# Mask products over 64 contraction rows, the base product split at column 256, lora's first product ahead of the attention values, mixing bias loaded group by group

## What is computed

```python
x = x + attn(cond(x, cond_128))          # per-sequence 32x32 mixing of tokens, then attention
x = x + ffn(conv(x, cond_128, fside))    # grouped conv of 9 taps, then a dense layer with lora experts

# cond: softmax of a small network of cond_128 weighs 8 matrices: out = agg_w @ x + agg_b
# attn: q, k, v = x @ Wq, x @ Wk, x @ Wv; rope on q and k; 32 query heads, 8 key heads of 16;
scores = jnp.einsum('bkgqd,bkmd->bkgqm', qg, k) / np.sqrt(HEAD_DIM)
scores = jnp.where(causal, scores, -jnp.inf)
out = jnp.einsum('bkgqm,bkmd->bkgqd', softmax(scores), v);  out @ Wo
# ffn:
base_out = jnp.einsum('btd,od->bto', x, base_W) + base_b
w = weights of the 8 best of 15 router classes, mapped to 8 experts
h = jnp.einsum('btd,erd->bter', x, A)
lora = jnp.einsum('bter,eor->bto', h * w[..., None], B) * 2
```

## Time and profile before

| | us |
|---|---|
| median of 3 runs | 644.11 |
| lowest, highest | 641.46, 644.9 |
| profiled execution, its own time | 646.57 |
| its span in the trace | 644.6 |

### The profile page before, as it was taken

How to read it: one execution, slowest core, us unless ns; L and a number is a source line. 1 busy time by engine, 2 the same in 40 slices (tenths; PEclk the granted TensorE clock), 3 DMA queues, 4 the chain that set the end, 5 groups by cost and what they waited for, 6 DMA issues and landing times.

```text
span 644.6 us, 14143 instructions
## 1 busy us (share of the span) xinstructions
PE 608.1 (94%) x4928; PEld 504.9 (78%) x4928; DVE 477.1 (74%) x1201; ACT 227.1 (35%) x635; POOL 223.8 (35%) x181
## 2 busy tenths in 40 slices
PE   4977996999999999999999999999999999999885
PEld 3665775888888888888888888888888888888664
DVE  3556565788778787878877878787887787878743
ACT  4342332333333343334333334333433333433310
POOL 6253131443333333344333333334433333333310
PEclk9979797999999999999999999999999999999989
DMA  7746346444344455444344445544533344444430
GB/s 172 123 133 135 88 105 152 124 116 108 88 95 104 102 122 122 122 122 122 97 99 92 100 102 122 122 122 122 122 96 99 90 102 103 122 122 106 107 82 34
DMA packets 121446, 71.23 MB, mean 110 GB/s; under 512 B 48357, under 2 KB 103301, under 8 KB 121176
## 3 DMA queue, kind: packets, MB, share of 16 engines
q1 hardware_dynamic: 119952, 70.53, 44.9%
q10 hardware_dynamic: 1336, 0.24, 0.2%
q0 software_dynamic: 144, 0.28, 0.2%
HBM read 51.49 MB, written 19.53 MB: 110 GB/s over the span
## 4 chain that ended last, share of the span: by engine, by line
PE 86%; DMA 5%; DVE 5%; issue 2%; SPq 1%; ACT 1%; POOL 0%; ACTq 0%; DVEq 0%
PE ps L415 20%; PE ps L566 15%; PE ps L593 9%; PE ps L587 8%; PE ps L613 5%; PE ps L605 5%; PE ps L515 4%; PE ps L632 4%; PE ps L552 4%; PE ps L654 3%; PE ps L621 2%; PE ps L577 2%; DMA scratch<-x_dram 2%; PE ps L555 1%; PE ps L601 1%
## 5 line engine op out<-in xcount | busy, mean ns | idle before, releaser
L941 POOL TENSOR_TENSOR qk<-network,t 128x640 f32<-128x640 f32 x31 | 48.3, 1558 | 161.7 <-DVE t L1118 161.7
L415 PE MATMUL ps<-wqkv_hi,y_hi 128*128 128x512 f32 (+1 forms) x256 | 89.4, 349 | 8.5 <-POOL y_lo L933 7.0
L415 PE MATMUL ps<-wqkv_hi,y_lo 128*128 128x512 f32 (+1 forms) x256 | 88.7, 346 | 0.0
L415 PE MATMUL ps<-wqkv_lo,y_hi 128*128 128x512 f32 (+1 forms) x256 | 88.5, 346 | 0.0
L953 POOL TENSOR_TENSOR raw<-x1p,basebB 128x512 f32<-128x512 f32 x32 | 49.3, 1541 | 64.9 <-DVE x1p L1193 64.9
L745 ACT ACTIVATE raw<-ps 128x512 f32<-128x512 f32 x64 | 37.8, 595 | 76.0 <-PE ps L632 75.9
L415 PEld LDWEIGHTS ps<-wqkv_hi,y_hi 128*128 128x128 f32 x256 | 49.7, 194 | 17.1 <-DVE raw L1137 9.2
L964 DVE TENSOR_TENSOR oT_lo<-ps,oT_hi 128x256 fp32r<-128x256 f32 x64 | 24.2, 419 | 50.4 <-ACT oT_hi L745 50.4
L948 POOL TENSOR_TENSOR raw<-raw,zero 128x512 f32<-128x512 f32 x32 | 33.2, 1039 | 79.6 <-DVE raw L1182 79.6
L807 ACT ACTIVATE raw<-raw 128x512 f32<-128x512 f32 x64 | 40.4, 632 | 54.9 <-DVE raw L1137 54.9
L925 POOL TENSOR_TENSOR raw<-raw,rz 128x512 f32<-128x512 f32 x32 | 33.6, 1049 | 65.6 <-DVE rz L1147 65.6
(11 more groups left out here) (182 smaller groups left out, 1485.4 us busy)
## 6 DMA issues: line engine op xcount, KB each, us to landing
scratch<-x_dram SPq DMA_DIRECT2D x96, 256.0 KB, 4.8
x_dram<-x1p SPq DMA_DIRECT2D x32, 260.0 KB, 2.1
xm<-x SPq DMA_DIRECT2D x32, 256.0 KB, 3.8
xr<-x SPq DMA_DIRECT2D x32, 256.0 KB, 2.7
out<-raw SPq DMA_DIRECT2D x32, 256.0 KB, 2.1
v_dram<-vS SPq DMA_DIRECT2D x32, 64.0 KB
vB<-v_dram SPq DMA_DIRECT2D x128, 16.0 KB, 4.2
mixb<-mixb_dram SPq DMA_DIRECT2D x1, 1280.0 KB, 7.7
```

The costliest lines, as they stand in the source:

```text
L415: last = mm(dst, a, b, start=(n == 0), stop=(n == 3 * len(left) - 1))
L941: nc.gpsimd.tensor_tensor(qk[:, :], t1, t2[:, :], ALU.add).then_inc(qk_sb, 1)
```

## The change

- The mask products use 64 contraction rows; DVE fills the 32 added rows of `query16` with zeros at the start.
- `BASE6` is 256: 12 products of 400 columns come first, then 12 of 256. DVE's adds follow these widths: `route2` adds 256 columns, `output` 256 and 256.
- `lora`'s first product (256 columns) becomes `lora_first`, between `conv` and `values`; the waits of `values` stand ahead of it. The product of 2 columns is gone. The other five stay after `values`.
- DVE copies the second half of `oT_hi`, ACT the first.
- `rawbase` is loaded ahead of the values of step 0; `prepare_base` (0, 1) moves to step 0 and (2, 3) to the place after `scores` in step 1.
- ACT and DVE split the router and A weights (`prepare_ar`) at the head of step 0; ACT copies the values there too, and starts Wo's split after `y_hi`, not ahead of the queries.
- `load_mixw(4, G)` moves from the end of step 0 to the end of step 1. `late_bias` is replaced by a load of 128 values per group, two steps ahead of its use, with a wait for the count in `next_y`.

The core of the diff:

```diff
-BASE6 = 3 * P
+BASE6 = 2 * P
...
             sp.dma_start(mixb[:, P:4 * P], mixb_row[P:4 * P].partition_broadcast(P)).then_inc(mixb_in, 16)
+            sp.dma_start(rawbase, baseW.rearrange("(p j) l -> p j l", j=PH)).then_inc(ld["base"], 16)
...
-            def late_bias(lo, hi):
+            def load_bias(u):
...
-                if peeled(t, 0):
+                if peeled(t, 1):
                     sp.wait_ge(mixw_out, 16)
                     load_mixw(sp, 4, G, mixw_in)
-                if peeled(t, 1):
-                    late_bias(4, 12)
-                if peeled(t, 2):
-                    late_bias(12, G)
+                if live(t + 3) and (not isinstance(t, int) or t > 0):
+                    load_bias(t + 3)
...
+            def lora_first(u):
                 pe.wait_ge(hwT_hi_sb, u + 1)
                 pe.wait_ge(hwT_lo_sb, u + 1)
+                if live(u + 2):
+                    values_ready(u + 2)
+                mm(ps[:, 6, 0:BASE6], hwT_hi[:, :], lora_hi[:, 0:BASE6], start=False, stop=False)
...
-                    rows = slice(h * P // 2, h * P // 2 + S)
+                    rows = slice(h * P // 2, (h + 1) * P // 2)
                     mm(ps[:, h, :], query16[rows, :], causal16[rows, :], start=True, stop=False)
...
-                if not isinstance(t, int):
-                    mm(ps[0:S, 4, 0:2], convW[:, 0, :, :].rearrange("p j o -> p (j o)"), xc[:, 0, 0:2], start=True, stop=True)
...
-                if peeled(t, 1):
+                if peeled(t, 0):
                     pe.wait_ge(prep_sb, 1)
                     prepare_base((0, 1))
+                if peeled(t, 1):
+                    prepare_base((2, 3))
...
-                if peeled(t, 1):
-                    pe.wait_ge(oT_lo_sb, 2)
-                    prepare_base((2, 3))
...
-                    for a in range(2):
-                        last = copy(heads(oT_hi, a), heads_ps(a))
-                    last.then_inc(oT_hi_sb, 1)
+                    copy(heads(oT_hi, 0), heads_ps(0)).then_inc(oT_hi_sb, 1)
...
+                if not isinstance(u, int) or u > 3:
+                    dve.wait_ge(mixb_in2, 16 * (u - 3))
...
+                v.tensor_copy(heads(oT_hi, 1), heads_ps(1)).then_inc(oT_hi_dve, 1)
```

More of the change, by code:

```diff
@@ L388, in steps @@
                     sp.dma_start(xr[:, :], group(x_g, t + 1)).then_inc(xr_in, 16)
-                if peeled(t, 0):
+                if peeled(t, 1):
                     sp.wait_ge(mixw_out, 16)
                     load_mixw(sp, 4, G, mixw_in)
-                if peeled(t, 1):
-                    late_bias(4, 12)
-                if peeled(t, 2):
-                    late_bias(12, G)
+                if live(t + 3) and (not isinstance(t, int) or t > 0):
+                    load_bias(t + 3)
             for t in range(0, 4):
                 steps(t)
-            with sp.Fori(4, G - 2) as t:
+            with sp.Fori(4, G - 3) as t:
                 steps(t)
-            for t in range(G - 2, G + 2):
+            for t in range(G - 3, G + 2):
                 steps(t)
@@ L560, in project @@
                 pe.wait_ge(oT_hi_sb, u + 1)
+                pe.wait_ge(oT_hi_dve, u + 1)
                 wait(pe, x1_sb, u)
@@ L586, in feed_forward @@
                 for n, (a, b) in enumerate(terms):
-                    last = mm(ps[:, 7, 0:P + NAR], a, b[:, BASE6:D + NAR], start=(n == 0), stop=(n == len(terms) - 1))
+                    last = mm(ps[:, 7, 0:D - BASE6 + NAR], a, b[:, BASE6:D + NAR], start=(n == 0), stop=(n == len(terms) - 1))
                 last.then_inc(ar_ps, 1)
@@ L713, in steps @@
                 if peeled(t, G):
+                    lora_first(t - 2)
                     lora(t - 2)
@@ L718, in steps @@
                     keep_warm(2)
+                if live(t - 2) and not peeled(t, G):
+                    lora_first(t - 2)
                 if live(t):
                     values(t)
-                if peeled(t, 1):
-                    pe.wait_ge(oT_lo_sb, 2)
-                    prepare_base((2, 3))
                 if live(t - 2) and not peeled(t, G):
@@ L850, in steps @@
                     act.wait_ge(ar_ps, t - 1)
-                    copy(arS[:, :], ps[:, 7, P:P + NAR]).then_inc(ar_sb, 1)
+                    copy(arS[:, :], ps[:, 7, D - BASE6:D - BASE6 + NAR]).then_inc(ar_sb, 1)
                 if live(t):
@@ L1160, in low_oT @@
             def low_oT(t):
+                dve.wait_ge(o_ps, t + 1)
+                v.tensor_copy(heads(oT_hi, 1), heads_ps(1)).then_inc(oT_hi_dve, 1)
                 dve.wait_ge(oT_hi_sb, t + 1)
-                for a in range(2):
-                    last = minus(heads(oT_lo, a), heads_ps(a), heads(oT_hi, a))
-                last.then_inc(oT_lo_sb, 1)
+                minus(heads(oT_lo, 0), heads_ps(0), heads(oT_hi, 0))
+                dve.wait_ge(oT_hi_dve, t + 1)
+                minus(heads(oT_lo, 1), heads_ps(1), heads(oT_hi, 1)).then_inc(oT_lo_sb, 1)
             def conv_bias(t):
```

67 lines of the change are left out of this document (35 added, 32 removed).

## The result

| | before | after |
|---|---|---|
| median of the runs (us) | 642.79 (640.13 to 644.9, 4 runs) | 634.59 (632.75 to 635.97, 4 runs) |
| ratio | | 0.9869, 95% interval 0.9842 to 0.9897 |
| profiled execution (us) | 646.57 | 635.97 |
| its span (us) | 644.6 | 634.2 |

What follows compares the result with a forecast made beforehand. PE bounds the loop (17.90 us a step); waits and low clock lengthen earlier steps. Loop -6.7, step 3 -8.2, step 1 -7.8, step 0 -0.8, step 2 +0.1, end +1.2: -22.2, median 621.9 us, range 616 to 632.

Steps and rivals of the forecast that it cites:

- Step 1: Step ahead of the loop: conv's input leaves 2.6 us earlier without the matrices, step ends at 65.0 instead of 72.81: -7.8 us.
- Masks: Loop, masks to scores: 64 rows remove a 0.09 us gap and 0.10 of unhidden weight load, 0.19 a step.
- Rival (a): Masks in the loop gain nothing or half, as the type changes there too: 624.7 to 627.3 us; chance 0.17.
- Step 2: Gets 448 KB of matrices ahead of its conv input and a 0.1 us longer router chain: +0.1, up to +1.
- Rival (b): Matrices delay step 2's conv input and values, PE stands 3 us, clock falls; 5 to 6 us back: 627.5; chance 0.10.
- Lora: Loop, conv to projection: values 0.20 us later, 0.21 less behind them; between -0.10 and +0.30, -0.05 taken.
- Rival (c): lora_first waits 0.3 us each loop step for hwT_lo or the copy, costing 9.8 us: 631.7; chance 0.08.
- Columns of the base product: Loop feed-forward, 400 and 256 columns: 0.04 us gain at most, 0 taken; router's result 0.7 us later, covered there.
- rival (e): Each step's 64 KB bias load pushes the conv's input past PE (margin 2.4 us), slower than before: 644 to 650; chance 0.02.
- Step 0: Start: reordered ACT work, masks and oT_hi's halves gain, 1 MB of base weights shares the DMA engines: -0.8 us taken.
- rival (d): Step 0 keeps full clock throughout, 2 to 3 us more gain: 619.5; chance 0.09.
- The end: Last steps: router's result 0.7 later, route2's add 0.1, lora 0.1 less, twice +1.4; step 31 gains 0.2: +1.2 us.

Runs made afterwards that it cites:

- b_masks64: The kernel before the change with only the masks of 64 rows and the zero rows' memset: 635.84 us, ratio 0.9896.
- mix_late: The changed kernel with the mixing matrices' four loads (groups 4 to 31) moved behind the load of v of step 2: 625.45 us, ratio 0.972.
- bias_behind: The changed kernel with each group's bias load moved behind the load of v of the same step: 624.99 us, ratio 0.9719.
- bias_early: As bias_behind, plus the wait for v moved ahead of the conv and the wait for hwT_hi left out: 623.17 us, ratio 0.968.
- no_first: The changed kernel without lora_first: all six lora products behind the values, the two-column product ahead of them: 624.33 us, ratio 0.9729.
- comb_384: The changed kernel without lora_first, matrices' and bias loads behind v, base product split 384 and 272 columns again: 620.07 us, ratio 0.966.
- early: The changed kernel with the wait for v moved ahead of the conv and the wait for hwT_hi left out: 643.1 us, ratio 0.9989.
- oT_act: As no_first, with oT_hi copied whole by ACT and both halves of oT_lo by DVE: 631.7 us, ratio 0.9846.
- comb_trim: The changed kernel without lora_first, matrices' and bias loads behind v, wait for v ahead of the conv: 615.51 us, ratio 0.9603.

## Why the prediction was right or wrong

**Step 1, right.** -7.8 forecast, -8.0 measured; all runs without the matrices in that place have 15.8 to 17.2. In the traces the conv starts 2.5 us earlier in the step (10.69 instead of 13.21), itself takes 0.9 less at full clock, and what follows it takes 4.1 instead of 8.7, without the second transposes and their wait of 1.61. No run moves the matrices without the transposes, so how the 8.0 divide between these edits is read from the traces and not tested.

**Step 3, right.** The wait for the wide bias load is gone, 17.97 us, and the one run with the old bias load has it still (b_masks64: 26.29).

**Masks, right.** 0.19 forecast, 0.20 to 0.21 measured by two opposite edits. Rival (a) is out: a change of type alone costs neither the gap nor the weights. By the Trainium skill, "TensorE: Matmul & The Clock Gate", Part 3, The mechanism, a weight load overlaps products in flight only where the row group differs, and 0.10 of the gain would have stayed away. Here the scores' loads start under the masks on the same 64 rows (308.37, 0.23 before the scores), so the measurement decides against it.

**Step 2, wrong: +0.1 taken, +7.1 measured.** This is the step of the working that failed most: the matrices' wait was put at next to nothing in the step that receives them. Rival (b) happened, at 0.10 of chance and with too low a price (5 to 6). Step 1 was judged by the load it loses, step 2 wasn't judged by the load it gets. The argument against, that the feed-forward stands ahead of the conv, was never worked out: in the changed kernel PE would have been ready for the conv about 13.5 us after the step's start (mix_late), the input left SP's queue 3.8 us later than in a loop step and lands at 17.2. With the matrices behind v the wait and the fall of the clock are gone (mix_late). It was also two loads, not one: the bias of the group was moved ahead of x and the conv's input too. With it behind v the input lands at 14.3 and 15.5 (bias_behind, bias_early) instead of 16.3 to 17.4, so it adds to the wait; of the delay against the 10.8 without either load in front, the matrices make the larger part (3.5 to 4.7 us). A wait above 2 us in step 2 is also one of the signs that the prediction named against itself. "Late next is nothing in sight" in the working of step 3 looked at who reads the matrices, and not at what queues behind their issue.

**Lora, wrong by 0.16 a step, and wrong in its bookkeeping.** Forecast +0.20 ahead of the values and -0.21 behind; measured +0.32 and -0.21. These two terms add to -0.01, yet -0.05 was taken: 0.04 had no priced term behind it, and the other 0.12 is the start of lora_first. The working had it start when conv and copies are done; but PE's sequencer still has three wait instructions of about 0.09 us each to run after hwT_lo, of which I had counted none. With one moved and one left out, it starts 0.12 earlier (bias_early). Rival (c) had the size wrong (0.35 a step) and the cause too: hwT_lo and the copy were done in time, at 319.33 and 319.43, and the weight load came at 319.66. The bookkeeping: the -0.21 stood in one sum with the product that was moved. Of it 0.10 are the 256-column products (0.91 to 0.81 in no_first) and 0.11 the product moved away (0.81 to 0.70), of which 0.06 are lost again in the projection (its first four products take 1.00 instead of 0.94). The part called "lora" was several edits in one sum: columns and halves of oT_hi bring 0.15 a step without lora_first (17.69 to 17.54), lora_first costs 0.23 (17.54 to 17.77).

**Columns of the base product.** 0 taken in the loop; comb_384 says 0.13: 0.03 in the feed-forward (the bound that I had worked out was 0.04), 0.10 in lora and 0.05 in the projection, less some 0.07 ahead of the values, where hwT_lo is ready earlier with the old columns.

**The bias load of each step, rival (e), mis-sized.** Its delay was put at 0.3 us from its share of the bytes (3%). It is 1.2 to 1.35 us. The margin of 2.4 us was read as the time from the last traffic to the conv, in one step; the median landing was 2.0 us ahead of the conv. What remains is 0.4, and it cost 0.4 us of waits over the loop. The rival's end (slower than before) didn't come, but early, with 0.65 us more in each step than bias_early, came to 0.9989 of the time before: the mechanism is real.

**Step 0, -0.8 forecast, +1.6 in this execution, not settled in size.** Nine further executions with this step 0, or with its base load in pieces, lie at 18.5 to 20.1 beside two of the old at 19.7, so about -0.4 is typical, near the forecast. The matrices of group 1 land 0.5 to 2 us later behind ACT's store than in the two kernels with the base weights a step later, which fits the load of the base weights as the reason. In two further runs (oT_act, bias_early) the clock stayed at 2.4 GHz through step 0, and it took 16.6 and 17.0: that is rival (d), true for some executions.

**The end, right in its mechanism.** 0.85 us more ahead of hw in each of the last two steps (1.13 to 1.98 in the last) against the forecast 0.8 (0.7 and 0.1). In the sum it is hidden, because the kernel before had 6.8 us at the low clock there and the changed kernel 3.4. Executions without that fall compare directly: from step 31 to the end 41.5 us in mix_late, early and bias_behind, 40.0 in b_masks64, which has the old columns and the new masks: +1.5 beside a forecast of +1.4 without the 0.2 of step 31.

The sum: 0.2 + 2.4 (step 0) - 0.2 (step 1) + 7.0 (step 2) + 0.3 (step 3) + 3.8 (loop) - 1.9 (end) = +11.7 (from unrounded terms) beside the forecast of -22.2, which gives the -10.5 of the spans. Of the loop's 3.8, some 3 are lora_first's late start and 0.4 waits for the conv's input. The 2.4 of step 0 and the -1.9 of the end are mostly differences between executions, so it is chance that they nearly cancel.

## What to carry to other kernels

A load that is moved away from one stage on a queue lands in another one: write down, for the stage that receives it, when each load behind it leaves the queue and when its reader is ready, before the gain of the first stage is counted. Count wait instructions as work of the engine that runs them, here about 0.09 us each where nothing runs under them, and put first those that are done long ago, but only if their margin has been read too. And take a term of several edits apart before it goes into the sum; here the one that named the change cost what the others brought.

## What the runs showed of the hardware that I had not expected

- A load of 64 KB whose 128 rows all read the same 512 bytes takes 3.8 us to land and makes the loads behind it on the queue 1.2 to 1.35 us later; behind v (3.3 us to land) the loop doesn't suffer from it (conv's input 10.57 instead of 11.74).
- Issuing the four loads of the matrices (896 rows of 128 bytes each) took SP 4.25 us in the changed kernel's step 2 and 3.27 in mix_late's, about 1 us each, where a load of x (xr, xm) took 0.43.
- On PE's sequencer a wait that computes its value costs about 0.09 us (319.48 to 319.57 to 319.66); one moved away gave 0.07 a step (comb_trim), one moved and one left out 0.10 (bias_early).
- The weights of a product load under one in flight on the same 64 rows (scores under masks, 308.37), but not across a change from 32 to 64 rows (317.01): 0.09 us of gap and 0.11 of load.
- Whether the clock falls around step 0 differs between executions of kernels that are nearly alike there: step 0 took 16.6 us (oT_act, clock 1.0 throughout) to 21.4 (the changed kernel, 0.76).
